# Third layer's attention steps moved into the counting passes of a four-layer graph network kernel, and 448 instead of 464 columns per block

## The reference, cut to what matters

```python
query = (x @ Wq_w + Wq_b).reshape(n, H, C)          # H = 2 heads, C = 128
key = (x @ Wk_w + Wk_b).reshape(n, H, C)
qs, ks = query / norm(query), key / norm(key)
terms = [x0]                                        # x, once for each head
for _ in range(K_ORDER):                            # 4 steps
    prev = terms[-1]
    gcn_i = segment_sum(prev[row], col) * deg_inv   # mean over a node's edges
    kvs = einsum('lhm,lhd->hmd', ks, prev)
    num = einsum('nhm,hmd->nhd', qs, kvs) + prev.sum(0)
    den = einsum('nhm,hm->nh', qs, ks.sum(0)) + n
    terms.append(BETA * gcn_i + num / den)
out = (concat(terms) @ Wo_w + Wo_b) / H
```

## Time and profile before

| what | value |
|---|---|
| runs | 6028.0 us median of 3 (6017.09 to 6033.16) |
| profiled execution, first to last instruction | 5325.0 us |
| its own time as a whole | not recorded apart; the median is 703 us above the span |
| PE / PEld / DVE / ACT / POOL busy | 81% / 57% / 53% / 27% / 61% |
| mean granted clock of PE | 0.918 of full |
| L1687, products with the counts | 992.8 us, 4,704 of them |
| L1601, gathers of the four steps | 617.7 + 499.1 us of POOL |
| L1673, sums of the gathered groups | 421.4 us, 3,552 |

### The profile page before, as it was taken

One profiled execution on the slowest core, in us unless ns is written; L12 is line 12 of the kernel. 1 busy time (PEld: TensorE's weight loads), 2 busy tenths in 40 slices (PEclk: granted clock), 3 DMA queues, 4 the chain that ended last, 5 costly groups with the idle time before them and its releaser, 6 DMA issues. The chain is left out here.

```text
span 5325.0 us, 78049 instructions
## 1 busy us (share of the span) xinstructions
PE 4321.5 (81%) x26640; PEld 3018.0 (57%) x26640; DVE 2815.1 (53%) x7430; ACT 1451.2 (27%) x2914; POOL 3251.7 (61%) x3382
## 2 busy tenths in 40 slices
PE   4677866979868787788879997999889767777786
PEld 3444434545535556554446664666555467667775
DVE  6588886755367776535562315221432444455554
ACT  1377850010057664111120102010210122222222
POOL 2766626767767775075516661776177367777774
PEclk6789988989989999699989998999999898999998
DMA  4265559999933344195588887988697465555553
GB/s 145 45 61 80 91 100 194 199 182 187 202 80 101 104 126 109 60 289 159 168 265 271 270 248 250 280 268 253 228 303 241 130 171 144 143 149 146 151 153 82
DMA packets 1261118, 909.00 MB, mean 171 GB/s; under 512 B 446403, under 2 KB 1181934, under 8 KB 1260638
## 3 DMA queue, kind: packets, MB, share of 16 engines
q1 hardware_dynamic: 909866, 519.09, 39.3%
q0 software_dynamic: 102704, 232.38, 16.1%
q10 hardware_dynamic: 248132, 152.25, 9.9%
HBM read 696.10 MB, written 118.89 MB: 153 GB/s over the span
## 5 line engine op out<-in xcount | busy, mean ns | idle before, releaser
L1687 PE MATMUL ps<-adj_d,xs_d 128*128 128x464 bf16 (+1 forms) x4704 | 992.8, 367 | 60.1 <-DVE xs_d L1648 60.1
L3166 POOL DMA_INDIRECT rows_mg<-p_tab,src_idx x784 | 758.3, 967 | 273.4 <-issue 238.1
L1601 POOL DMA_INDIRECT rows_d<-xh_tab,src_idx x632 | 617.7, 977 | 479.8 <-POOLq L187 207.4
L1601 POOL DMA_INDIRECT rows_d<-x_tab,src_idx x512 | 499.1, 975 | 475.5 <-POOLq L187 264.4
L1687 PEld LDWEIGHTS ps<-adj_d,xs_d 128*128 128x128 bf16 x4704 | 466.1, 101 | 509.1 <-DVE xs_d L1648 61.9
L1295 POOL DMA_INDIRECT rows_d<-h_tab,slot_idx x490 | 497.0, 1014 | 266.9 <-issue 143.9
L2216 POOL DMA_INDIRECT rows_g<-x_tab,src_idx x444 | 434.2, 978 | 164.7 <-issue 127.3
L3263 PE MATMUL ps<-win_mg,turned_hot_mg 128*128 128x128 f32 x1568 | 341.2, 302 | 201.2 <-DVE pre_mg L3215 201.0
L1431 PE MATMUL ps<-adj_d,xs_d 128*128 128x512 bf16 (+1 forms) x2028 | 441.0, 375 | 54.6 <-DVE xs_d L1396 49.9
L1673 PEld LDWEIGHTS ps<-onehot_d,rows_d 128*128 128x128 f32 x3552 | 428.6, 192 | 66.6 <-DVE onehot_d L1619 33.5
L1673 PE MATMUL ps<-onehot_d,rows_d 128*128 128x72 f32 (+1 forms) x3552 | 421.4, 275 | 31.3 <-DVE onehot_d L1619 26.3
(11 more groups left out here) (442 smaller groups left out, 7541.4 us busy)
## 6 DMA issues: line engine op xcount, KB each, us to landing
adj_d<-adjacency SPq DMA_DIRECT2D x140, 812.0 KB
adj_d<-adjacency SPq DMA_DIRECT2D x84, 857.5 KB
attr_mg<-in_edge_attr SPq DMA_DIRECT2D x195, 256.0 KB
xp_g<-x_tab SPq DMA_DIRECT2D x70, 448.0 KB
k_rows_d<-k_tab ACTq DMA_DIRECT2D x56, 448.0 KB
loc_mg<-loc_rows SPq DMA_DIRECT2D x196, 128.0 KB
q_s<-q_tab SPq DMA_DIRECT2D x42, 448.0 KB
rden_s<-rden_tab SPq DMA_DIRECT2D x42, 448.0 KB
```

The costliest lines, as they stand in the source:

```text
L1601: nc.gpsimd.indirect_dma_start(rows[:, q % GR * K + k, :], None, table, bass.IndirectOffsetOnAxis(ap=src_idx[:, j:j + 1], axis=0)).then_in ...
L1687: last = nc.tensor.matmul(ps[:, m % 2, 0:w], xs[:, g * GW + k, e, :], adj[:, slot, k, 0:w], start=(g == 0 and k == 0 and e == 0), stop=(g ...
L3166: nc.gpsimd.indirect_dma_start(rows[:, q % RR, k, :], None, p_tab, bass.IndirectOffsetOnAxis(ap=src_idx[:, j:j + 1], axis=0)).then_inc(row ...
```

## The change

`layer2_step` is gone. `dense_pass` takes a further argument: a `Step` whose work is cut into 14 visits of 512 or 384 columns, two for each node group (`NODE_PARTS`). A list of slots, written out by a planner, takes the place of `due` and `gathered`: each slot has the pieces, gather groups, tile, `ask` and `finish` that all engines execute in it. Pieces now run ahead, two to a slot with one head and one with two, from the first slots on; visits open when the pieces are through (with two heads also not before tile 42), each as soon as its columns' block is stored and its groups are summed. The planner counts time with `TILE_US`, `GROUP_US`, `GATHER_US`, `PIECE_US`, `VISIT_US`, and takes up to two groups in a slot.

In a slot PE does: pieces, `ask`, groups, tile, `finish`. All loads and stores of a visit are on ACT's queue. Results with two heads are written over the sums in `acc`; buffers are the free plane of `planes` (one head), or `raw`, the keys' buffers and 1 MB more (two). With two heads there is one buffer for share and rden. Step 1 first stores `xT` (`x_kept`, 3,136 KB), so that the way out can restart (`step_again`). Two-head passes get 448 columns per block and 82 groups. Both heads' sums of a group now share a PSUM bank. Tables alternate (`xh_tab`, `xh2_tab`).

```diff
-SPLITS = {1: Split(6, 490, 528), 2: Split(5, 464, 468)}
+SPLITS = {1: Split(6, 490, 528), 2: Split(5, 448, 456)}
+TILE_US, GROUP_US, GATHER_US, PIECE_US, VISIT_US = {1: 4.5, 2: 4.1}, {1: 0.9, 2: 1.75}, 5.05, {1: 2.4, 2: 1.6}, 4.3
...
+                        while t < tiles or q < groups or finished < PARTS_N:
+                            took = pieces[p:p + per_slot] if t or heads == 1 else []
+                            opens = p >= len(pieces) and (heads == 1 or t >= free_at)
+                            p += len(took)
+                            group = []
+                            while q < groups and len(group) < 2 and clock > 4.5 + GATHER_US * (q + 1):
+                                group.append(q)
+                                q += 1
+                            tile = t if t < tiles else None
+                            able = [v for v in ready if needs(*v)[1] <= q and (needs(*v)[0] < 0 or stored_at(needs(*v)[0]) < t or tile is None)]
+                            ask = finish = None
+                            if opens and able:
+                                ask = len(visits)
+                                visits.append(able[0])
+                                ready.remove(able[0])
+                            if tile is not None:
+                                finish = ask
+                            elif finished < len(visits) - (ask is not None):
+                                finish = finished
...
+                def begin(self, act, again=False):
+                    if again:
+                        act.dma_start(xT[:, 0:NP], x_kept).then_inc(self.kept, 16)
+                    elif keeps:
+                        act.dma_start(x_kept, xT[:, 0:NP]).then_inc(self.kept, 16)
+                    self.load_q(act, 0)
+                    for i in range(1 + self.deep):
+                        self.load_rest(act, i)
+                    self.load_q(act, 1)
...
+                def load_rest(self, act, i):
...
+                        elif not self.deep and i:
+                            act.wait_ge(self.made, HEADS * i)
+                        act.dma_start(self.share[b][:, 0:w], dinv_row[c:c + w].partition_broadcast(P)).then_inc(self.rest_in[b], 16)
+                        for h in range(HEADS):
+                            act.dma_start(self.rden[b][h][:, 0:w], rden_tab[h * P:(h + 1) * P, c:c + w]).then_inc(self.rest_in[b], 16)
...
+                def ask(self, eng, i, finished=0, again=False):
...
+                        if finished:
+                            eng.wait_ge(self.copied, HEADS * finished)
+                        for h in range(HEADS):
+                            nc.tensor.matmul(ps[:, 4 + h, 0:w], kv[:, h, :], self.q[i % 2][h][:, 0:w], start=True, stop=True).then_inc(self.asked, 1)
...
+                    elif not self.deep:
+                        self.load_rest(eng, i + 1)
...
+                def finish(self, eng, i, bank, again=False):
...
+                            eng.wait_ge(self.made, HEADS * i + h + 1)
+                            x = self.result(i, h)
+                            for k in range(nw):
+                                done = nc.tensor.transpose(ps[:, bank + h, k * P:(k + 1) * P], x[:, k * P:(k + 1) * P], ident[:, :])
+                            done.then_inc(self.turned, 1)
...
+                        for h in range(HEADS):
+                            done = nc.tensor.matmul(ps[:, 6 if last else 6 + i % 2, 0:w], wt(WO[h][step]), self.result(i, h), start=(h == 0), stop=(h == HEADS - 1))
...
+                            nc.scalar.copy(self.rows[h][:, 0:w], ps[:, bank + h, 0:w]).then_inc(self.copied, 1)
...
-            dense_pass(f"2{step}", table, heads, SPLITS[heads], phases)
-            general_pass(f"2{step}", table, heads, src_index, dst_target)
-            if step < ORDER:
-                layer2_step(step)
+            make = fused_step(step, to, step == 1)
+            dense_pass(f"2{step}", table, heads, SPLITS[heads], phases, make)
+            again = step_again(make, step < ORDER - 1)
+            general_pass(f"2{step}", table, heads, src_index, dst_target, nodes=lambda tmp: again(tmp, heads))
+        dense_pass(f"2{ORDER}", x_tab, 1, SPLITS[1], [[keys_values(xh_tab, HEADS, 2, PARTS_N)], [LastAttention]])
+        general_pass(f"2{ORDER}", x_tab, 1, src_index, dst_target)
```

More of the change, by code:

```diff
@@ L45 @@
 BATCH = 14
+NODE_PARTS = [(g * GC + half * BLOCK, GW - BW if half else BW) for g in range(G) for half in range(2)]
+PARTS_N = len(NODE_PARTS)
+Slot = namedtuple("Slot", "pieces groups tile ask finish")
+TILE_US, GROUP_US, GATHER_US, PIECE_US, VISIT_US = {1: 4.5, 2: 4.1}, {1: 0.9, 2: 1.75}, 5.05, {1: 2.4, 2: 1.6}, 4.3
 MOST = 256
@@ L1483, in dense_pass @@
                         at += len(work.signals)
+                    if step:
+                        step.take(*s[at:])
                     tiles = heads * blocks * G
@@ L1508, in dense_pass @@
[L1508 to L1513, removed]
-                    def beside(eng, t):
-                        for before, piece in due[t]:
+                            for k in range(most):
+                                pieces.append([(work, k, g) for work in phase if work.parts == most] +
+                                              [(work, 0, g) for work in phase if work.parts < most and k == most // 2])
@@ new lines, in dense_pass, with stored_at, needs @@
+                    pieces = [(phases[opened.index(k) - 1] if k and k in opened else (), piece) for k, piece in enumerate(pieces)]
+                    def stored_at(m):
+                        return order.index((m + 1, 2) if m else (1, G - 1)) if m < heads * blocks - 1 else tiles
+                    def needs(c, w):
+                        first_block = (heads - 1) * blocks
+                        covering = [first_block + b for b in range(blocks) if b * block_of < c + w]
+                        g = c // GC
+                        of_dense = c + w <= blocks * block_of
+                        sums = 0 if of_dense else groups if g == G - 1 else max(0, FINAL[g] - tail // K)
+                        return covering[-1] if c < blocks * block_of else -1, sums
@@ L1518, in beside @@
+                    if step:
+                        slots, visits = fused_slots()
+                        step.visit(visits)
+                        begins = min(k for k, slot in enumerate(slots) if slot.ask is not None)
+                    else:
+                        slots = even_slots()
+                    first_idle = min(k for k, slot in enumerate(slots) if slot.tile is None)
+                    def beside(eng, slot):
+                        for before, piece in slot.pieces:
                             for work in before:
```

481 lines of the change are left out of this document (287 added, 194 removed).

## The result

The changed kernel takes **6118.9 us** (median of 4 runs, 6089.5 to 6121.9), the kernel before beside it 6026.4 (6017.1 to 6033.2): ratio 1.0147, 95% interval 1.0123 to 1.017, some 92 us slower. The forecast was 6039, its upper end 6100. Two single executions in the later groups, of 7802 and 16351 us, were slow ones at a mean clock of 0.74 and 0.63, and enter no ratio.

A forecast was written before the change was run, and what follows sets the result against it. PE was taken to bound the two-head passes, DMA a close second, and latency the attention step. Step 1 at -8, step 2 at +9.4 and step 3 at +9.6 made +11 on 6028.0: 6039 us, range 5980 to 6100.

The forecast's parts named there:

- 703 us above the span, and assume that this rest stays: Whole kernel: median of 6028.0 us against a profiled span of 5325.0, the difference carried over unchanged.
- Keys and values: Two-head passes, slots 1 to 14: PE waits for single-buffer loads, 9.5 us from piece to piece, about 18 us per pass.
- The rival of the single buffer: Two-head passes, slots 1 to 14: loads need 10 us, waits of 54 us, +36 per pass, 6111 us; chance 0.18.
- Visits in the two-head passes: Step 2: attention products +52.8 us, waits inside visits 16, tail 7, against the removed attention step of 79.6.
- The ask behind ACT's copy: Two-head visits following each other: PE's next ask waits for ACT's copy of turned rows, 1.2 us more each.
- Step 1: One-head pass with its attention: 477 us against 485, 8 us less, some 20 us either way for the queries.
- The x_kept wait: Step 1, before the first ask: the first visit's loads wait behind the 3.2 MB store, 13 us, between 0 and 18.
- Columns: Two-head passes: 448 columns save 9.9 us in tiles, three more groups cost 5.2, net 4.7 us won per pass.
- The steps by my own marks: First tile to next pass's first load: some 477, 542 and 560 us for steps 1, 2 and 3.
- the forecast's mechanism: Two-head passes: waits of the moved loads eat the latency won, 6015 to 6065 us; chance 0.43.

The follow-up runs named there:

- hybrid: Kernel before with only step 1 fused as in the change, its x_kept store issued behind the first visit's loads: ratio 1.0013 to before, +8 us.
- steps23: Kernel before with steps 2 and 3 fused as in the change, step 1 as before, x_kept store left out: ratio 1.0114 to before, +70 us.
- no_kept_store: Changed kernel without the x_kept store in step 1: ratio 1.0018 to the kernel before.
- early_one: Kernel before with 448 columns and the 14 two-head pieces of keys and values in slots 1 to 14, one buffer, no visits: ratio 1.0131, +66 us.
- pieces_apart: Changed kernel with the two-head passes' pieces of keys and values in every second slot: ratio 1.014 to the kernel before.
- wide: Changed kernel with two-head pieces some 2.9 slots apart (slots 1 to 38), x_kept store behind the first visit's loads: 5297.9 us against 5329.9, ratio 0.9942.
- early_two: early_one with a second buffer for the rows of keys and x in the two-head passes: ratio 1.0066 to the kernel before, +29 us.

## Why the prediction was wrong

**The step that failed first** is "703 us above the span, and assume that this rest stays". Beyond the span lie 1.7 us. The 703 were the other condition, spread over all stages as late issue. A sum from durations of the quick trace is a sum for the quick condition. There the change costs 21 us where the sum has 11; in the condition that was timed it costs 92. In that one the steps whole are +8 (hybrid) and +70 (steps23) where the sum has -8 and +19; the 14 us between 78 and 92 lie between groups and in the moved store, and aren't assigned.

**Keys and values: the term had the wait and left out the clock.** The sum put "about 18 us" on each two-head pass. The pieces alone cost 66 us for two passes in the quick condition and 80 in the late one, in place of 36. In the changed kernel itself PE waited less than forecast, in step 2 of the quick trace

```profile
PE ps L2673 <- DMA kx_rows_d<-xh_tab: 11.4, 5, 4.3
```

and 13.5 us in step 3 (10.0 and 12.4 in no_kept_store). What the sum put at nothing is the work at the lower clock behind these waits: by the same groups' durations at full clock I estimate 16 and 5 us there, 7 and 19 in no_kept_store. Waits and clock together are some 24 us a pass, and taking the pieces apart won about 25. In early_one, where the groups aren't packed into these slots, the waits are 24.0 and 18.2 us. The period was somewhat short: pieces start 11.1, 9.2 and 10.6 us apart (2816.13, 2827.24, 2836.45, 2847.06) where the sum has 9.5. Also left out was the first load beside that for splitting, which I had in the earlier trace rows and used for the rival's end alone. The rival of the single buffer named the mechanism and the place; its 54 us were too many, and it too counted waits only. Its second argument, the Trainium skill's rule that a DMA engine goes round between queues (DMA: Bandwidth & Descriptors, "Queues, rings and completion order"), had led me to an estimate of 9 us for a pair under full traffic; loads issued at 2829.40 and 2838.72 had PE going 7.1 and 8.3 us later, at a DMA share of 0.90, and the one of 2803.29 took 12.8, so these traces neither bear it out nor refute it.

**Visits in the two-head passes: right in sign, the size open.** Forecast with their tail against the removed step: 52.8 + 16 + 7 - 79.6 = -4 in step 2, and -4 in step 3. Changed kernel less early_one, by the traces: 566.8 - 570.8 = -4.0 and 578.2 - 588.0 = -9.8; with no_kept_store in the first place, -18.5 and -2.5. By the times the visits gain some 30 us for both. Between these I can't decide, and the planner also places the gather groups otherwise, so it isn't the visits alone. A tile took 3.97 us (3.98 forecast). The ask behind ACT's copy came as forecast in kind but at 5.3 us for step 2, where 11 visits at 1.2 us make 13.

**Step 1: right in the quick condition, as far as one pair of traces tells.** -8 forecast, -10 measured. The x_kept wait was 9.9 us and its removal 13, forecast 13. As an estimate, the Trainium skill's fit for one DMA of the other kind of queue (same page, "Anatomy of one DMA") made it 9.4 us under way; it was 11.1, beside other traffic, so the fit is too low here. That step 1 gains nothing in the late condition no step of mine could say.

**Columns: right that they win little.** 5 us per pass forecast; the traces show 5 to 12 in one group, the times nothing.

**The steps by my own marks, quick.** From first tile to the next pass's first load the changed kernel took 475, 557 and 565 us, forecast 477, 542 and 560. That the forecast's +11 came within 10 us of the +21 measured is in part luck: the pieces cost more than their term, and the visits gained more than theirs.

**What the late condition adds.** Pieces alone: 80 us there (464 columns), 66 in the quick one, and 24.1 and 24.0 us of waits for rows in step 2, 8 of them in each. Steps 2 and 3 whole: 70 there, 36 in the quick one by the traces. So the pieces lose about as much in both, and what the visits win back in the quick condition is mostly gone in the late one. That late issue takes it is an inference from differences of groups and traces, and not shown; why taking the pieces apart wins 14 us or less there and some 50 in the quick condition is open too (pieces_apart has them 2 slots apart, wide 2.9), as is why instructions come late at all.

So the forecast's mechanism held, a single buffer whose loads PE waits for, but its price left out the clock, and it was set in a condition that no case of mine contained: every rival was worked out on the same 703 us.

## What to carry to other kernels

Compare the span of a profile with the times beside it before anything else: where hundreds of us lie between them, the trace may be of another condition, and differences hold only within one. When work moves earlier to make room for a fusion, space it over all the slots up to the first one that needs it: dense prefetching through one buffer cost 33 us a pass, and 2.9 slots between the pieces won some 25 of it back in the quick condition. Price a wait on PE together with the slower work that can stand behind it (here about as much again in the changed kernel), and an added fusion by its parts run alone: here the part that looked like bookkeeping was the whole loss.

## What I had not expected of the hardware

- The same kernel takes 5329 to 5338 or 6030 to 6067 us, and within one group of runs it doesn't change. POOL's gather is 966 and 964 ns, DVE's busy time 2815 and 2800 us, the first queue's packets 2113 and 2121 us; only the start of instructions is late, and PE's mean clock is 0.86 in place of 0.92.
- The instruction queues aren't it in any way that the profile shows: their packets are 0.3% and 0.1% of the DMA engines' time in both conditions.
- The length of a wait alone doesn't say what the work behind it takes. In step 2 of early_one waits of 1.8 and 2.8 us were followed by pieces of 1.83 us, one of 3.1 us by 2.95 and one of 9.3 us by 3.35, in place of 1.72; in early_two one of 1.9 us was followed by 2.90.
